# Two gated transformer layers on one core: a pair's flags reduced on GpSimd, sums taken out of the small bank by ScalarE, expert weights streamed, new orders

## The reference

```python
x = x + tanh(g_xattn[0]) * L0_xattn(layernorm(x), ctx)   # 16 heads of 8, softmax over all 1601 keys
x = x + tanh(g_ffn[0])   * L0_ffn(layernorm(x))          # 8 experts 128->512->128, gelu, top 2 by router
x = x + tanh(g_xattn[1]) * L1_xattn(layernorm(x), ctx)   # softmax over the 32 greatest of 1601 scores
x = x + tanh(g_ffn[1])   * L1_ffn(layernorm(x))          # self attention + 8 linear experts, top 2
```

## Time and profile before

| | us |
|---|---|
| median of 3 runs (lowest, highest) | 4908.51 (4906.88, 4911.69) |
| the profiled execution's own time | 4911.92 |
| its span, first to last instruction | 4910.1 |
| busy: PE, DVE, ACT, POOL | 4268.7, 4203.5, 4014.6, 1312.9 |
| mean granted TensorE clock, share of full | 0.955 |
| DMA: bytes; share of 16 engines | 332.13 MB; 28.7% (the data queue) |

### The profile page before, as it was taken

The page is one execution under the profiler, slowest core; times in us unless marked ns, Lnnn a source line. Parts: engine busy times, 40 slices in busy tenths (PEclk is TensorE's granted clock), DMA queues, the critical chain, the costliest instruction groups (busy, mean ns, idle before and its releaser), DMA issues. The chain is left out here.

```text
span 4910.1 us, 108232 instructions
## 1 busy us (share of the span) xinstructions
PE 4268.7 (87%) x33307; PEld 2101.1 (43%) x33862; DVE 4203.5 (86%) x22712; ACT 4014.6 (82%) x5260; POOL 1312.9 (27%) x2809
## 2 busy tenths in 40 slices
PE   5879779999798999889889999997999799998775
PEld 2435235453443535344443535444353444534222
DVE  5478998989989898998989899898989989888782
ACT  2558778989798898879879898997989699898774
POOL 3121222232223223222322333232232223122121
PEclk7889999999999999999999999999999899999887
DMA  5332232323233233323323332332333233131110
GB/s 133 77 81 64 64 69 62 79 63 80 56 77 78 60 74 72 77 59 78 79 48 77 70 88 61 77 83 53 72 73 83 53 76 76 44 70 34 36 29 21
DMA packets 356926, 332.13 MB, mean 68 GB/s; under 512 B 102659, under 2 KB 313750, under 8 KB 356310
## 3 DMA queue, kind: packets, MB, share of 16 engines
q1 hardware_dynamic: 356310, 324.86, 28.7%
HBM read 217.55 MB, written 107.13 MB: 66 GB/s over the span
## 5 line engine op out<-in xcount | busy, mean ns | idle before, releaser
L991 DVE MAX8 cand<-s 128x8 f32<-128x67 f32 (+1 forms) x12288 | 1974.9, 220 | 106.2 <-ACT s L943 92.0
L962 ACT ACTIVATE prob<-wide 128x1024 f32<-128x1024 f32 (+1 forms) x1792 | 1780.8, 1025 | 209.8 <-PE wide L656 80.9
L1077 DVE TENSOR_REDUCE part<-score 128x1 f32<-128x512 f32 x1536 | 1017.9, 677 | 213.7 <-PE score L610 134.4
L656 PE MATMUL wide<-q,k_att 128*128 128x256 bf16 (+1 forms) x6656 | 1008.8, 277 | 78.5 <-ACT prob L962 25.0
L702 PE MATMUL att<-prob,v 128*9 128x256 f32 (+1 forms) x14336 | 1044.8, 383 | 12.6 <-ACT prob L962 7.3
L943 ACT ACTIVATE s<-wide 128x1024 f32<-128x1024 f32 (+1 forms) x1024 | 844.7, 842 | 137.9 <-PE wide L630 130.9
L952 ACT ACTIVATE below<-wide 128x1024 bf16<-128x1024 f32 (+1 forms) x832 | 819.6, 1025 | 100.8 <-PE wide L656 95.9
L656 PEld LDWEIGHTS wide<-q,k_att 128*128 128x128 bf16 (+1 forms) x6656 | 557.8, 99 | 531.0 <-ACT prob L962 182.7
L610 PE MATMUL score<-k_scan,q 128*128 128x512 bf16 x1313 | 501.3, 393 | 189.7 <-DVE part L1077 114.5
L1309 POOL TENSOR_SCALAR flag<-cand,ends 128x24 bf16<-128x24 f32 x512 | 185.6, 363 | 1636.4 <-DVE ends L1016 1518.7
L678 PE MATMUL wide<-below,minus_ident 128*128 128x512 bf16 x1515 | 474.0, 388 | 137.0 <-ACT below L952 62.7
(11 more groups left out here) (169 smaller groups left out, 5257.2 us busy)
## 6 DMA issues: line engine op xcount, KB each, us to landing
k_scan<-k_stack SPq DMA_DIRECT2D x512, 150.1 KB, 3.3
k_stack<-split_b SPq DMA_DIRECT2D x576, 128.0 KB, 2.7
k_att<-k_stack SPq DMA_DIRECT2D x384, 192.0 KB, 3.6
ctxT<-in_ctx_dram SPq DMA_DIRECT2D x32, 800.5 KB, 5.8
q_stack<-split_b SPq DMA_DIRECT2D x192, 64.0 KB, 2.1
q<-q_stack SPq DMA_DIRECT2D x128, 96.0 KB
self_stack<-split_b SPq DMA_DIRECT2D x192, 64.0 KB, 2.0
k_self<-self_stack SPq DMA_DIRECT2D x64, 96.0 KB
```

What stands on the lines that cost most here:

```text
L656: r = tensor.matmul(ps[0:kc, j * S:(j + 1) * S], m.k_att[kn % 3][:, j, c0:c0 + kc], rows[:, j, :], start=(j % 2 == 0), stop=(l == 0), skip ...
L962: scalar.activation(pr[0:kc, :], ps[0:kc, :], ACT.Exp, scale=SCALE).then_inc(sem["wide_done"], 1)
L991: i = vector.max(cand[:, :, c], s[:, KCUT[c]:KCUT[c + 1]])
L1077: vector.tensor_reduce(m.part[:, QT * hh + qt, c:c + 1], score[i % 2][:, :], AX.X, ALU.max).then_inc(sem["score_max"], 1)
```

## The change

- `flag` is gone from TensorE. `look` moves to GpSimd and takes the maximum over all partitions and columns of the flags itself, into one of two cells `many`.
- The sums leave `small` by a new ScalarE step `o_take` (128 x 72 elements into one of two buffers `weighed`), which is now the drain of `u_turn`. `o_rec` on VectorE reads SBUF; `o_norm` moves to GpSimd, and so does `ln_scale`.
- Layer 0's expert weights are loaded per batch and expert into 3 buffers, by a new SP step `w_in` (two DMAs of 256 KB); `v_w1` waits for it. 5 `prob` buffers instead of 3, 4 `hid` buffers instead of 2.
- `z_score` reads all 128 rows of its operands, where it read 48; `kq_in` has a third DMA which first sets the three appended rows of q to zero.
- All five word lists of `ORDER`, and `LAG`, are new. `NARROW` is used nowhere.

```diff
@@ constants
+PROBS = 5
+HIDS = 4
+WBUF = 3
@@ ORDER, pool (one line of nine; the other lists are new in the same way)
-        mark shift.0 split.w_k.1 mark*4 shift.1 ln_pow.z mark*2 split.z_qk*2 mark ln_pow.v mark z_add mark shift.0
...
+        mark shift.0 split.w_k.1 mark look mark*2 look o_norm.1 mark shift.1 ln_pow.z ln_scale.z mark look mark
...
@@ small_drain
             if name == "u_turn":
-                return "o_norm", key
+                return "o_take", key
...
-            if name == "mix_bias":
-                return "mix_start", key
-            return "look", key
+            return "mix_start", key
@@ tensor: v_w1 (v_w2 reads m.w_2[n % WBUF])
-                        ps = fill(name, *key)
+                        ps, n = fill(name, *key), E * b + e
+                        q.wait_ge(w_in[n % WBUF], 32 * (n // WBUF + 1))
@@ tensor: z_score
-                            r = tensor.matmul(score[i % 2][:, t * S:(t + 1) * S], q_self[0:ROWS, h, t * P:(t + 1) * P],
-                                              k_self[0:ROWS, h, :], start=True, stop=True)
+                            r = tensor.matmul(score[i % 2][:, t * S:(t + 1) * S], q_self[:, h, t * P:(t + 1) * P],
+                                              k_self[:, h, :], start=True, stop=True)
-                    elif name == "flag":
-                        g, pair = key
-                        ps = claim(name, *key)
-                        q.wait_ge(sem["marked"], after("mark", scan_tile(g, 2 * pair + 1)))
-                        tensor.matmul(ps[0:1, 0:QT * (KC + 1)], m.ones_col[:, :], flat(m.flag),
-                                      start=True, stop=True).then_inc(sem["small_full"], 1)
@@ scalar
-                    if n >= 3:
-                        q.wait_ge(sem["pv_done"], n - 2)
-                    return m.prob[n % 3]
+                    if n >= PROBS:
+                        q.wait_ge(sem["pv_done"], n - PROBS + 1)
+                    return m.prob[n % PROBS]
...
+                    elif name == "o_take":
+                        n = turn("take", name, *key)
+                        q.wait_ge(sem["small_full"], after("u_turn", *key))
+                        if n >= 2:
+                            q.wait_ge(sem["o_done"], after("o_norm", *takes[n - 2][1]))
+                        scalar.activation(m.weighed[n % 2][:, :, :, :].rearrange("p t j r -> p (t j) r"),
+                                          small[:, 0:QT * P].rearrange("p (c r) -> p c r", r=32)[:, :, 0:HD + 1],
+                                          ACT.Copy).then_inc(sem["taken"], 1)
@@ vector
-                    elif name == "look":
-                        q.wait_ge(sem["small_full"], after("flag", *key))
-                        if before("check", *key):
-                            q.wait_ge(sem["checked"], before("check", *key))
-                        vector.tensor_reduce(m.many[:, :], small[0:1, 0:QT * (KC + 1)], AX.X,
-                                             ALU.max).then_inc(sem["looked"], 1)
...
+                        q.wait_ge(sem["taken"], after("o_take", *key))
+                        if n >= 2:
+                            q.wait_ge(sem["o_done"], after("o_norm", *takes[n - 2][1]))
+                        vector.reciprocal(m.rec[n % 2][:, :, :], m.weighed[n % 2][:, :, :, HD]).then_inc(sem["inverted"], 1)
@@ gpsimd
+                        for t in range(QT):
+                            i = gpsimd.tensor_tensor(o[:, t, :, :], pv[:, t, :, 0:HD],
+                                                     rec[:, t, :].unsqueeze(2).to_broadcast([P, HG, HD]), ALU.mult)
...
+                            i = gpsimd.tensor_scalar(m.xn[:, t, :], m.x[b % 5][:, t, :], m.mv[:, t, 0:1],
+                                                     m.rstd[:, t:t + 1], ALU.subtract, ALU.mult)
...
+                    elif name == "look":
+                        g, pair = key
+                        n = HG * g + pair
+                        q.wait_ge(sem["marked"], after("mark", scan_tile(g, 2 * pair + 1)))
+                        if n >= 2:
+                            q.wait_ge(sem["checked"], after("check", *divmod(n - 2, HG)))
+                        gpsimd.tensor_reduce(m.many[pair % 2][:, :], flat(m.flag), AX.XYZWC, ALU.max).then_inc(sem["looked"], 1)
@@ sync
+                    elif name == "w_in":
+                        b, e = key
+                        n = E * b + e
+                        if n >= WBUF:
+                            q.wait_ge(sem["small_full"], after("v_w2", (n - WBUF) // E, (n - WBUF) % E))
+                        sync.dma_start(m.w_1[n % WBUF][:, :], a["L0_ffn_W1"][e, :, :]).then_inc(w_in[n % WBUF], 16)
+                        sync.dma_start(m.w_2[n % WBUF][:, :, :],
+                                       a["L0_ffn_W2"][e, :, :].rearrange("(t p) d -> p t d", p=P)).then_inc(w_in[n % WBUF], 16)
...
+                        sync.dma_start(q_self[ROWS:ROWX, :, :], q_self[64:64 + ROWX - ROWS, :, :]).then_inc(kq_in[g % 2], 16)
```

More of the change, by code:

```diff
@@ L46 @@
 KB = 4
+NARROW = ("pv", "pv_z")
+PROBS = 5
+HIDS = 4
+WBUF = 3
 TILES = 6
@@ L85 @@
     pe="""
-        pv.1 w_k.0 rw_turn.v c1 n0 c1 mix_bias.v n0 s_1 v_w2 s_1 n0 cut_add v_w2 cut_add z_score c1 pv.1 flag c1 s_1
-        pv.1 c1 cut_add n0 row_turn.2 pv.1 n0 v_w1 pv.1 v_w1 n0 row_turn.1 n0 c1 v_w2 s_0 n0 c1 n0 v_w2 s_0 pv.0 s_0
-        n0*2 c1 flag pv.0 s_0 w_v.0 u_turn.1 n0 s_0 v_w1*2 ln_turn.w n0 pv.0*3 s_0 n0*2 c1 v_w2 w_k.0 s_0 pv.0 s_0
-        n0*2 s_0 pv.0*2 w_q s_0 n0 s_0 pv.0 c1 v_w2 s_0 v_w1*2 z_score flag pv.0*2 c1 v_w2 s_0 s_z n0 v_w2 s_z n0
-        pv.0*2 s_1 n0 s_1 pv_z*2 cut_add u_turn.0 z_score*2 cut_add w_v.0 z_score c1 u_turn.2 s_1 n0 s_1 pv.1
@@ new lines @@
+        pv.1 w_k.0 rw_turn.v c1*2 mix_bias.v n0 s_1 v_w2 s_1 cut_add n0*2 v_w2 cut_add z_score c1 pv.1 c1 n0 s_1
+        pv.1 row_turn.2 c1 cut_add pv.1 n0 v_w1*2 n0 pv.1 row_turn.1 n0 c1 v_w2 w_v.0 n0*2 s_0 v_w2 c1 n0 w_k.0 s_0
+        pv.0 s_0 n0 s_0 pv.0 n0 c1 u_turn.1 s_0 z_score v_w1 n0 v_w1 ln_turn.w pv.0*3 s_0 n0 v_w2 s_0 n0 c1 n0 pv.0
+        w_q n0 c1 n0 s_0 n0 s_0 pv.0*2 s_0*2 v_w2 s_0 v_w1*2 pv.0*3 c1 v_w2 s_0 n0 s_z v_w2 s_z z_score pv.0*2 s_1*2
+        pv_z*2 cut_add u_turn.0 n0*2 cut_add w_v.0 z_score c1 z_score s_1 n0 s_1 u_turn.2 pv.1 cut_add n0 cut_add
@@ L169 @@
     pe={
-        "cut_add": 146, "c1": 160, "pv.1": 148, "n0": 79, "row_turn.0": 3, "s_1": 146, "w_k.1": 4, "flag": 41,
-        "s_0": 52, "w_v.1": 4, "u_turn.1": 12, "pv.0": 52, "o_turn.1": 3, "row_turn.1": 11, "o_proj.1": 3,
-        "ln_turn.z": 3, "z_v": 3, "u_turn.0": 4, "o_turn.0": 1, "route.z": 3, "z_qk": 6, "o_proj.0": 1, "z_moe": 6,
-        "ln_turn.v": 1, "route.v": 1, "z_score": 61, "w_k.0": 0, "v_w1": 14, "v_w2": 16, "row_turn.2": 16,
-        "w_v.0": 0, "ln_turn.w": 0, "w_q": 0, "s_z": 32, "pv_z": 32, "u_turn.2": 16, "ln_turn.u": 2, "u_q": 2,
@@ L175 @@
-        "rw_turn.v": 2, "mix_bias.v": 2, "rw_turn.z": 3, "mix_bias.z": 3},
+        "cut_add": 146, "c1": 160, "pv.1": 148, "n0": 79, "row_turn.0": 3, "s_1": 146, "w_k.1": 4, "s_0": 52,
+        "w_v.1": 4, "u_turn.1": 12, "pv.0": 52, "o_turn.1": 3, "row_turn.1": 11, "o_proj.1": 3, "ln_turn.z": 3,
+        "z_v": 3, "u_turn.0": 4, "o_turn.0": 1, "route.z": 3, "z_qk": 6, "o_proj.0": 1, "z_moe": 6, "ln_turn.v": 1,
+        "route.v": 1, "z_score": 61, "w_k.0": 0, "v_w1": 14, "v_w2": 16, "row_turn.2": 16, "w_v.0": 0,
@@ L258, in streams @@
     for l in range(3):
-        for name in ("row_turn", "row_minus", "shift", "rows_out", "rows_in", "u_turn", "o_rec", "o_norm", "att_copy"):
+        for name in ("row_turn", "row_minus", "shift", "rows_out", "rows_in", "u_turn", "o_take", "o_rec", "o_norm", "att_copy"):
             of(f"{name}.{l}", name, [(l, g) for g in groups])
@@ L266, in streams @@
     of("mark", "mark", [(n,) for n in range(QT * HG * NG)])
-    for name in ("flag", "look", "check"):
+    for name in ("look", "check"):
         of(name, name, [(g, hh) for g in groups for hh in range(HG)])
@@ L289, in streams @@
         of(f"{name}.z_qk", name, [("z_qk", b, n) for b in batches for n in range(2)])
-    for name in ("v_w1", "v_gelu", "v_w2", "v_add"):
+    for name in ("w_in", "v_w1", "v_gelu", "v_w2", "v_add"):
         of(name, name, [(b, e) for b in batches for e in range(E)])
@@ L360, in build @@
     copies = T.number("act", "att", ("att_copy",))
-    norms = T.number("dve", "norm", ("ln_scale",))
+    takes = T.number("act", "take", ("o_take",))
+    norms = T.number("pool", "norm", ("ln_scale",))
     assert norms == [("ln_scale", k) for n, k in T.steps["dve"] if n == "ln_stats"]
@@ L414, in build @@
         m.flag = sb("flag", [P, QT, KC + 1], BF16)
-        m.many, m.size, m.th = sb("many", [1, 1], I32), sb("size", [P, HG * QT]), sb("th", [P, HG * QT])
+        m.many = [sb(f"many{n}", [1, 1], I32) for n in range(2)]
+        m.size, m.th = sb("size", [P, HG * QT]), sb("th", [P, HG * QT])
         m.part = sb("part", [P, HG * QT, 4])
```

293 lines of the change are left out of this document (143 added, 150 removed), and 2 rows, old and new, of the table sp.

## The result

The changed kernel takes 4927.33 us (median of 8 runs, 4921.49 to 4934.43), the kernel before 4910.12 (8 runs, 4906.88 to 4914.14): ratio 1.0035, 95% interval [1.0025, 1.0046]. Forecast were 4815 and a range up to 4925, so the direction was wrong and the range was left by 2 us. The span of the profiled execution is 4932.6 us, 22.5 more than before.

A forecast was written before the change was run, and what follows sets the result against it. It took a ring of three engines with TensorE slightly ahead as the bound. Nine terms summed to -93.5 us, from the profiled 4911.9 to 4818.4; with the runs' median 3.4 lower it predicted 4815 us, range 4730 to 4925.

The forecast's parts named there:

- Term 1: The flag step leaves TensorE: 47.5 us of its own and 21.0 us idle before it go, -68.5 us.
- Term 3: VectorE loses multiplications, looks and layer norm, about 179 us of its queue; TensorE's waits let -30 us of it count.
- Rival B: VectorE is the pacing engine, so all its 179 us come off: about 4745 us or near 4730; chance 13%.
- Term 4: ScalarE gets `o_take`, 192 copies at 300 ns, 57.6 us in all, half put on the path: +29 us.
- Terms 2 and 5: TensorE's small-bank waits end as ScalarE drains `u_turn`, -11 us; ScalarE's waits for weighings end with five prob buffers, -16.
- Term 6: GpSimd takes multiplications, 161 us, and layer norm steps, 52 us; almost nothing waits for them directly, cost 0.
- Term 7: The look's maximum on GpSimd takes under 4.5 us, so VectorE's check does not wait for it: no cost.
- rivals A and E: Slow GpSimd look holds up VectorE: 8 us gives 5144, chance 9%; column by column, some 6 us, gives 4920, 8%.
- Term 8: Loads on SP: streamed expert weights and tighter `k_att` cost +13 us, earlier scan loads give back 8: +5 together.
- Term 9: Start and tail: fewer weights at the start -5 us, last outputs through more engines +3; the wider `z_score` 0.
- TensorE slightly ahead: In a ring of three engines TensorE leads, so its work counts in full, VectorE's only through TensorE's waits, ScalarE's in part.
- Rival C: ScalarE paces, so the copy's +58 us counts in full and only -16, -11, -5 besides: 4935 us; chance 7%.

The follow-up runs named there:

- K: The changed kernel with one `kq_in` in SP's order moved to the end of the pass before, transfers untouched: 4892.72 us, ratio 0.9961 to the kernel before.

## Why the prediction was wrong, by its own steps

**Where the gain went.** From before: the GpSimd maximum -3, wide `z_score` with its third transfer -5, everything else together (copy, GpSimd's multiplies, buffers, streamed weights, new orders) -9 (4901.47 to 4892.72), `kq_in`'s place +35: 4927. Without the last these are -17, where the forecast's sum was -93.5. So of the 112 us between forecast and result 77 are a gain that never was there, and 35 a cost that was not counted. The first part is all in the flag and the look: some -82 by the forecast's terms, -3 measured. What the forecast had for the rest, -11.5, is near the -14 that were measured, but by terms of both signs that no run took singly, so that agreement is luck until shown.

- **Term 1 (flag, -68.5) failed, and with it the forecast.** It took a group's 47.5 us of busy time as time on the path, by the premise that work off TensorE counts in full; its queue share is 4 to 7 us (16 to 26 ns x 256), and 1024 products more cost 6 us. It took the 21.0 us of idle time as saved. Measured with the look: -3. Where the idle time went stays open.
- **Term 3 (VectorE relieved, -30).** Its 138.7 us were groups' busy times; VectorE's whole busy time fell by 105. At VectorE's share of 0.14, measured on K, that is 15. Rival B (179 in full) is refuted by the same number, and by the looks: out of VectorE's queue they gave 3 us.
- **Term 4 (`o_take`, +29).** Forecast 300 ns, measured 243; in its orders the copy gives instead of costing (67 us slower without). By ScalarE's slope its 47 us alone would be 27.
- **Terms 2 and 5 (-11, -16).** The small bank's waits and ScalarE's wait for weighings named there are gone from the rows, and no gain of that size is to be seen. Four prob tiles in place of five changed nothing; three weren't tried.
- **Term 6 (GpSimd at 0): no row speaks against it, and its prices were off both ways.** The multiplications took 239 ns in place of 420, the layer norm steps 792 in place of 410, the group 101 us where I had 52. TensorE's wait for `xn` went from 19.9 to 23.3.
- **Term 7 (look) held:** 397 ns for 128 x 50 over all axes, and 16.3 us of VectorE's waits for `many` in the kernel with this part alone. The 6.05 us that I had worked out by columns from a figure of the Trainium skill (GPSIMD Engine Reference, "Cross-partition") is refuted by this row, and rivals A and E with it. The page's own figure, for 128 x 2048, no run here tests.
- **Term 8 (loads, +5) failed by an omission.** Streaming itself came out near its size (13 forecast, some 12 estimated from a 6 that isn't told from nothing), and `v_w1` did not wait for its weights: its group sat idle 5.4 us in all, 4.8 of them for ScalarE. But I costed the moved order for `k_att`, `w_in` and `k_scan` and not for `kq_in`, of which I counted only the issues. +35.
- **Term 9, `z_score` at 0:** -5 to -13 with its third transfer, of which only the 13 is clear.
- **"TensorE slightly ahead"** was the root of it. Rival C (ScalarE paces, 7%) named the engine whose cut gave most; that its 4935 came near is luck, since its +58 for the copy has the wrong sign in these orders and the +35 of `kq_in` isn't in it.

## What to carry to other kernels

A matmul's mean in a group is its length, not its price: compare the groups' sum with the engine's busy time, or issue it several times over. Before comparing two traces, compare their counts: where matmul records are missing, the same wait stands in other rows. Before summing gains on a kernel whose engines are all over 80% busy, take a known piece of work from each engine in turn, and run each often enough; here the shares were 0.13, 0.14 and 0.57, the first two hardly told from 0. When a load order is redrawn, cost every load in it against what now stands ahead of it in the same queue; one word moved behind an 800 KB transfer cost 35 us, and all else in the change gave 17.
